# Eight transfers in place of sixteen for the turned shift, issued one key block sooner

## The chip, the cores and the metric

The program runs on one core of one Trainium2 chip. Its time is the device time of that core in microseconds (us). The core has a matrix engine (TensorE, PE in the profile), a vector engine (VectorE, DVE), a scalar engine (ScalarE, ACT), GpSimd (POOL) and a queue that does nothing but issue transfers (SyncE, SP). SBUF is the core's on-chip memory with 128 partitions, PSUM its accumulator memory with eight banks.

## The reference, cut to what matters

```
x = x + attention(layernorm(x))      # 2 sequences x 2048 tokens x 256, 16 heads of 16
x = x + experts(layernorm(x))        # router, 2 of 4 experts per token

scores = Q @ K^T / 4
A = softmax(scores)
out = (0.6 * A + 0.4 * L) @ V        # L: a fixed band of 7 neighbours
out = out @ Wo^T + bo
```

The change touches the attention alone, of which there are 2 x 16 = 32 heads with 2048 x 2048 scores each. The softmax needs the largest score of every query, so that the exponential is taken of score minus maximum.

## The kernel before, in words

The 32 heads are worked one after the other, each as 16 key blocks of 128 keys (`kb` in the code). For one head and one key block TensorE computes four chunks of scores, each 128 keys x 512 queries (L748), ScalarE takes their exponential into `probs` (L696), and TensorE multiplies with the values (L760). Scores lie with keys on the partitions, and so the maximum of a query cannot be subtracted there by a per-partition operand. It goes into the matmul: the stack `score_q` has three times 16 rows of query pieces and two more rows (rows 48 and 49) with minus the maximum of each query, in a high and a low piece; `score_k` holds ones in those rows. Two copies of the stack lie in the partitions from 0 and from 64 (`ROW_TILES = 2`, `ROW_TILE = 64`): queries 0 to 1023 in the first, 1024 to 2047 in the second.

The maxima are found one head ahead, from a second set of scores with queries on the partitions: TensorE fills two banks (L738), VectorE reduces them (L638), two reductions a key block. Maxima run `LOOK - ST` = 5 blocks ahead of the scores, so that the 16 blocks of head n+1 are done in the key block `kb == 10` of head n. There VectorE writes `neg_max` (L646), GpSimd splits it into `shift` (L604, L606), and at `kb == SHIFT_AT` VectorE turns it with 32 x 32 transposes into `shift_tok` (L654). SyncE then moves pieces of `shift_tok` into the two extra rows of `score_q` (L493); it is 128 bytes from each of some partitions of `shift_tok` to one row. TensorE waits for all of it before the first scores of the next head, which it computes in `kb == 15` (the wait on `shift_in`, L814).

SyncE's queue is in order. For head n it goes: loads of the maximum stacks for head n+2 (L528), the gather of head n's softmax sums (L530, 4 transfers by L147), a pad, a weight chunk's store and load, the inverse of the sums out and back (L536 to L538), the head's result (L540), the shift of head n+1 (L543), and, after the last scores of head n (`s_ready`, L545), the loads of the score stacks for head n+2 (L546), 12 transfers like the maximum stacks' 12. VectorE inverts the gathered sums in `kb == INVERT_AT` = 3 of the next head (L658), in the midst of its reductions. The queues of all engines are written out by hand in this order; a loop body holds six heads.

Of the kernel before, what the change touches and what calls it, by code (L numbers as in the profile page):

```python
# [7 lines left out]
F32 = mybir.dt.float32  # L8
# [8 lines left out]
P = 128  # L17
# [9 lines left out]
ST = SEQ // P  # L27
# [7 lines left out]
PIECES = 2  # L35
# [3 lines left out]
STACK = HD * len(Q_ROWS)  # L39
SROWS = STACK + PIECES  # L40
ROW_TILES = 2
ROW_TILE = P // ROW_TILES
# [3 lines left out]
WIN = P + 2 * WINDOW  # L46
BAND = BT * WIN + 2 * WINDOW
LOOK = 21
SHIFT_AT = 12
INVERT_AT = 3  # L50
PROBS = 4
SIX = 6
QUAD = 32
# [29 lines left out]
def ds(start, size):  # L83
    return bass.ds(start, size)


def by_head(engine, body):

    rounds = (NHEADS - 1) // SIX
    with engine.Fori(0, rounds) as i:  # L90
        for k in range(SIX):
            body(SIX * i + k, SIX // 2 * i + k // 2, k, False)
    for n in range(rounds * SIX, NHEADS):
        body(n, n // 2, n - rounds * SIX, n == NHEADS - 1)
# [24 lines left out]
def load_max(sp, dram, q_stack, k_stack, n, signal):  # L119
    load_stack(sp, dram, 0, Q_ROWS, q_stack, n, False, signal)  # L120
    load_stack(sp, dram, 1, K_ROWS, k_stack, n, True, signal)


def load_score(sp, dram, q_stack, k_stack, n, signal):
    load_stack(sp, dram, 0, Q_ROWS, q_stack, n, True, signal)
    load_stack(sp, dram, 1, K_ROWS, k_stack, n, False, signal)
# [17 lines left out]
def gather_sums(sp, keep, signal):  # L144

    for c in range(BPS):
        sp.dma_start(keep["sum_tok"][QUAD * c:QUAD * (c + 1), :],  # L147
                     keep["heads_sb"][QUAD * c + HD:QUAD * c + HD + 1, :].rearrange("o (t q) -> o t q", q=ST)
                     ).then_inc(signal, 16)


def store_inverse(sp, dram, keep, signal):

    sp.dma_start(dram["inv"].rearrange("(p t) -> p t", t=ST), keep["inv_tok"][:]).then_inc(signal, 16)


def spread_inverse(sp, dram, keep, signal):

    for c in range(BPS):
        row = dram["inv"][c * BLOCK:(c + 1) * BLOCK].rearrange("(o f) -> o f", o=1)  # L160
        sp.dma_start(keep["inv_rows"][QUAD * c:QUAD * c + HD, :], row.partition_broadcast(HD)).then_inc(signal, 16)


def store_head(sp, dram, keep, place, signal):

    for c in range(BPS):
        sp.dma_start(dram["o"][ds(place, 1), :, c * BLOCK:(c + 1) * BLOCK].squeeze(0),
                     keep["heads_sb"][QUAD * c:QUAD * c + HD, :]).then_inc(signal, 16)


def load_heads(sp, dram, keep, i, signal):

    b, q0 = i // BPS, (i % BPS) * BLOCK
    for m in range(KD):
        head = 1 + b * HEADS + m * (HEADS // KD)
        sp.dma_start(keep["o_block"][i % 2][:, m, :],
                     dram["o"][head:head + HEADS // KD, :, q0:q0 + BLOCK].rearrange("h d t -> (h d) t")
                     ).then_inc(signal, 16)
# [215 lines left out]
def attend(nc, ctx, dram, keep, block):  # L394
# [8 lines left out]
    def sb(name, shape, dt=F32):  # L403
        return ctx.enter_context(nc.sbuf_tensor(name, shape, dt))

    def sem(name):
        return ctx.enter_context(nc.semaphore(name))
# [4 lines left out]
    score_q = [sb(f"score_q{u}", [STACK_ROWS, SPLIT], F32R) for u in range(2)]  # L412
# [8 lines left out]
    part_max, neg_max, shift, shift_tok = (keep[n] for n in ("part_max", "neg_max", "shift", "shift_tok"))  # L421
# [11 lines left out]
    def count_of(n, kb, c):  # L433
        return n * UNITS + CH * kb + c + 1

    def bank_of(k, kb, c):

        return ps_s[(k * UNITS + CH * kb + c) % RING]
    SHIFT_DMAS = PIECES * ROW_TILES * P // QUAD
    PARTS = 2  # L440

    ones_set = sem("ones_set")
# [10 lines left out]
    shift_in = [sem(f"shift_in{u}") for u in range(2)]  # L453
# [30 lines left out]
    @block.sync  # L484
    def _(sp):
        def load_shift(u):

            for q in range(P // QUAD):
                for c in range(PIECES):
                    for h in range(ROW_TILES):  # L490
                        row, first = h * ROW_TILE + STACK + c, QUAD * q + c * ST + h * ST // ROW_TILES
                        to = score_q[u][row:row + 1, :].bitcast(F32).rearrange("o (t q i) -> o t q i", q=P // QUAD, i=QUAD)
                        sp.dma_start(to[:, :, q, :], shift_tok[first:first + ST // ROW_TILES, :]  # L493
                                     ).then_inc(shift_in[u], 16)

        load_max(sp, dram, max_q[1], max_k[1], 1, max_in[1])
        sp.wait_ge(ones_set, SCORE_ONES)
        load_score(sp, dram, score_q[0], score_k[0], 0, score_in[0])
        load_score(sp, dram, score_q[1], score_k[1], 1, score_in[1])
        for dst, src in ((w_o[:], dram["woT"].rearrange("(k p) n -> p k n", p=P)),  # L500
                         (w_r1[:], dram["rW1"].rearrange("(k p) n -> p k n", p=P)),
                         (w_r2[:], dram["rW2"].rearrange("(k p) n -> p k n", p=P)),
                         (b_r1[:], dram["rb1"]),
                         (bias_o[:], dram["bo"].rearrange("(o f) -> o f", o=1).partition_broadcast(P))):
            sp.dma_start(dst, src).then_inc(route_in, 16)
        sp.wait_ge(shift_tr, 1)
        load_shift(0)
        sp.dma_start(keep["band"][:], dram["band"][0]).then_inc(keep["band_in"], 16)

        def load_chunk(n):  # L510
            sp.dma_start(w_raw[:], dram["we"][ds(n, 1)].squeeze(0)).then_inc(w_in, 16)

        def store_chunk(n):
            sp.wait_ge(w_lo, n + 1)
            sp.dma_start(dram["w_split"][ds(n, 1)].squeeze(0), w_pair[:].bitcast(F32)).then_inc(w_stored, 16)

        def pad_slots(n):
            sp.dma_start(dram["xs"][ds(n * SLOTS, SLOTS), :], dram["pads"]).then_inc(pads_in, 16)

        pad_slots(NHEADS)  # L520
        sp.dma_start(dram["out"][TOKENS:, :], dram["pads"][:, 0:DIM]).then_inc(pads_in, 16)
        load_chunk(0)

        def body(n, h, k, last):
            u, more = k % 2, not isinstance(n, int) or n + 2 < NHEADS
            if more:
                sp.wait_ge(m_ready, 2 * ST * (n + 1))
                load_max(sp, dram, max_q[u], max_k[u], n + 2, max_in[u])  # L528
            sp.wait_ge(o_copied, n + 1)
            gather_sums(sp, keep, sums_in)  # L530
            pad_slots(n)
            store_chunk(n)
            if not last:
                load_chunk(n + 1)
            sp.wait_ge(inv_ready, n + 1)
            store_inverse(sp, dram, keep, inv_out)  # L536
            sp.wait_ge(inv_out, 16 * (n + 1))
            spread_inverse(sp, dram, keep, inv_in)  # L538
            sp.wait_ge(scaled, n + 1)
            store_head(sp, dram, keep, n, o_out)  # L540
            if not last:
                sp.wait_ge(shift_tr, n + 2)
                load_shift(1 - u)  # L543
            if more:
                sp.wait_ge(s_ready, count_of(n, ST - 1, CH - 1))  # L545
                load_score(sp, dram, score_q[u], score_k[u], n + 2, score_in[u])  # L546

        by_head(sp, body)
        sp.wait_ge(o_out, 16 * BPS * NHEADS)
        for i in range(2):  # L550
            load_heads(sp, dram, keep, i, keep["heads_in"][i])
# [81 lines left out]
    def _(dve):  # L633
# [7 lines left out]
        def split_shift(m, u):  # L641

            dve.wait_ge(m_read, 2 * ST * (m + 1))
            if not isinstance(m, int) or m > 0:
                dve.wait_ge(shift_ready, m)
            nc.vector.tensor_reduce(neg_max[:], part_max[:, u], axis=AXIS.X, op=ALU.max, negate=True  # L646
                                    ).then_inc(shift_step, 1)

        def transpose_shift(m, loaded, loads):

            dve.wait_ge(shift_ready, m + 1)
            if loaded is not None:
                dve.wait_ge(loaded, 16 * SHIFT_DMAS * loads)
            nc.vector.transpose(shift_tok[:], shift[:].rearrange("p c t -> p (c t)").bitcast(F32)).then_inc(shift_tr, 1)  # L654
# [17 lines left out]
        def body(n, h, k, last):  # L672
            u = k % 2
            for kb in range(ST):
# [5 lines left out]
                if ahead == ST - 1 and not last:  # L680
                    split_shift(n + 1, 1 - u)
                if kb == SHIFT_AT and not last:
                    transpose_shift(n + 1, shift_in[u], h + 1)
# [47 lines left out]
    def _(pe):  # L731
# [52 lines left out]
        for t in range(LOOK):  # L784
# [3 lines left out]
            for p in range(2):  # L788
                half = 2 * t + p
                maxima(t, t % ST, t // ST, p)  # L790
                if half == FIRST_SCORES:
                    pe.wait_ge(v_copied, BANKS - 1)
                    pe.wait_ge(score_in[0], 16 * STACK_DMAS)
                    pe.wait_ge(shift_in[0], 16 * SHIFT_DMAS)
                if half >= FIRST_SCORES:
# [5 lines left out]
        def body(n, h, k, last):  # L801
            u = k % 2
            pe.wait_ge(v_in, n + 1)
            for kb in range(ST):
# [7 lines left out]
                if kb == ST - 1 and more_scores:  # L812
                    pe.wait_ge(score_in[1 - u], 16 * STACK_DMAS * (h + 1 + u))
                    pe.wait_ge(shift_in[1 - u], 16 * SHIFT_DMAS * (h + 1 + u))  # L814
                if more_scores:
# [929 lines left out]
```

## Time and profile before

| | |
|---|---|
| time, median of 3 runs | 2596.38 us (2569.75 to 2608.95) |
| profiled execution | 2588.01 us, span 2586.2 us |
| TensorE busy | 2261.4 us (87%) |
| VectorE busy | 1641.1 us (63%) |
| ScalarE busy | 1351.8 us (52%) |
| mean granted TensorE clock | 0.806 of full |

The span is the time from the first to the last instruction of the profiled execution. Busy time counts an engine's own instructions; what it waits for stands in the view of waits, and the granted clock of a stretch in the view by windows (1.00 is 2.4 GHz, 0.50 is 1.2 GHz). The heads take up most of the span: the shift is turned for the first at 118.4 us and for the last at 1941.8 us. What follows them is the output projection, the router and the experts.

### The profile page before, as it was taken

How to read it: one execution, taken by the hardware profiler on the slowest of the kernel's cores; microseconds unless marked ns; L12 is line 12 of the kernel's file. 1: busy time of each engine (PE TensorE's matmuls, PEld its weight loads, DVE VectorE, ACT ScalarE, POOL GpSimd, SP SyncE). 2: the span in 40 equal slices, each digit the busy share in tenths (PEclk: the TensorE clock that was granted, in tenths of full speed). 3: DMA queues.
4: the chain of work that ended last, by engine and by line, in shares of the span. 5: the costliest groups of instructions: out<-in, count | busy, mean ns of one | idle time of the engine just before them, and what ended most of it. 6: DMA issues, size and time to landing. Idle time of an engine off the chain costs nothing. (4 is left out here: it accounts for less than half of the span.)

```text
span 2586.2 us, 48018 instructions
## 1 busy us (share of the span) xinstructions
PE 2261.4 (87%) x16092; PEld 1100.5 (43%) x16092; DVE 1641.1 (63%) x2123; ACT 1351.8 (52%) x2390; POOL 367.9 (14%) x380
## 2 busy tenths in 40 slices
PE   8988888888887888888887888888889699999998
PEld 4532333232232233322332332322332577999997
DVE  6766667566577676766776666676770377655554
ACT  3255666456566565665665555565666144222322
POOL 1440000000000000000000000000000046222222
PEclk9977778667688777887877677786876799999999
DMA  7723443233333354333333333443311237778885
GB/s 250 179 72 74 75 91 70 62 65 63 63 63 63 74 86 82 71 65 64 63 63 64 62 68 74 75 92 64 66 45 38 70 126 282 230 236 272 283 275 147
DMA packets 133884, 279.86 MB, mean 108 GB/s; under 512 B 43616, under 2 KB 74336, under 8 KB 126944
## 3 DMA queue, kind: packets, MB, share of 16 engines
q1 hardware_dynamic: 120464, 258.65, 40.0%
q0 software_dynamic: 13152, 17.83, 3.5%
q8 instruction: 144, 2.36, 0.4%
q14 instruction: 124, 1.02, 0.2%
HBM read 215.40 MB, written 78.54 MB: 114 GB/s over the span
## 5 line engine op out<-in xcount | busy, mean ns | idle before, releaser
L638 DVE TENSOR_REDUCE part_max<-psum 128x1 f32<-128x1024 f32 x1024 | 1242.2, 1221 | 584.1 <-PE psum L738 579.0
L696 ACT ACTIVATE probs<-psum 128x512 f32<-128x512 f32 x2048 | 1114.1, 595 | 739.0 <-PE psum L748 690.7
L748 PE MATMUL psum<-score_q,score_k 50*128 50x512 f32 x2048 | 923.2, 543 | 256.7 <-DMA score_q<-shift_tok 245.6
L738 PE MATMUL psum<-max_k,max_q 48*128 48x512 f32 x2048 | 895.3, 536 | 16.1 <-DVE part_max L638 16.0
L760 PE MATMUL psum<-probs,v_ones 128*32 128x256 f32 x8192 | 819.8, 480 | 0.5 <-ACT probs L696 0.2
L748 PEld LDWEIGHTS psum<-score_q,score_k 50*128 50x128 f32 x2048 | 379.1, 229 | 828.2 <-ACT probs L696 545.9
L760 PEld LDWEIGHTS psum<-probs,v_ones 128*32 128x32 f32 x8192 | 177.3, 119 | 474.6 <-issue 366.0
L738 PEld LDWEIGHTS psum<-max_k,max_q 48*128 48x128 f32 x2048 | 358.6, 226 | 32.8 <-DVE part_max L638 24.1
L1154 ACT ACTIVATE x_sb<-psum,x_sb 128x512 f32<-128x512 f32 (+1 forms) x160 | 101.5, 635 | 253.9 <-PE psum L1550 253.8
L1569 PE MATMUL psum<-w,h_hi 128*128 128x256 f32 x1120 | 203.0, 280 | 0.0
L1569 PEld LDWEIGHTS psum<-w,h_hi 128*128 128x128 f32 x1120 | 179.4, 189 | 10.3 <-DVE h_lo L1365 0.2
L1569 PE MATMUL psum<-w,h_lo 128*128 128x256 f32 x560 | 156.4, 279 | 0.0
L1363 DVE CAST h_hi<-x_sb 128x512 fp32r<-128x512 f32 (+1 forms) x160 | 66.6, 416 | 129.1 <-ACT x_sb L1154 128.8
L611 POOL TENSOR_TENSOR heads_sb<-heads_sb,inv_rows 128x512 f32<-128x512 f32 x32 | 40.9, 1278 | 640.0 <-DMA inv_rows<-inv 640.0
L1569 PEld LDWEIGHTS psum<-w,h_lo 128*128 128x128 f32 x560 | 105.6, 189 | 0.0
L1365 DVE TENSOR_TENSOR h_lo<-x_sb,h_hi 128x512 fp32r<-128x512 f32 (+1 forms) x160 | 100.3, 627 | 5.5
L572 POOL COPY v_ones<-v_sb 128x256 f32<-128x256 f32 x32 | 12.7, 396 | 629.6 <-PE psum L760 629.5
L1550 PE MATMUL psum<-xT_hi,w 128*128 128x512 f32 (+1 forms) x320 | 93.9, 375 | 2.2 <-ACT x_sb L1154 2.2
L1550 PE MATMUL psum<-route_xT_hi,w 128*128 128x512 f32 (+1 forms) x320 | 90.3, 364 | 0.0
L1102 POOL DMA_INDIRECT out<-x_sb,token x36 | 56.8, 1578 | 136.5 <-DVE x_sb L1383 82.0
L1102 POOL DMA_INDIRECT out<-attnT,token x34 | 53.4, 1570 | 140.2 <-DVE attnT L1383 92.7
L1074 POOL DMA_INDIRECT xs<-xrow,slot_at x64 | 63.3, 990 | 22.6 <-issue 18.4
(177 smaller groups left out, 1250.8 us busy)
## 6 DMA issues: line engine op xcount, KB each, us to landing
w<-w_split SPq DMA_DIRECT2D x40, 2048.0 KB, 8.5
max_q<-qk_pieces SPq DMA_DIRECT2D x192, 128.0 KB, 6.9
score_k<-qk_pieces SPq DMA_DIRECT2D x192, 128.0 KB, 4.6
xs<-in_pads SPq DMA_DIRECT2D x33, 528.0 KB, 5.6
qk_pieces<-pieces SPq DMA_DIRECT2D x32, 512.0 KB, 4.8
w_split<-w_pair SPq DMA_DIRECT2D x32, 512.0 KB, 6.1
max_k<-qk_pieces SPq DMA_DIRECT2D x192, 64.0 KB, 7.9
score_q<-qk_pieces SPq DMA_DIRECT2D x192, 64.0 KB, 2.2
```

What stands on the lines that cost most here:

```text
L638: nc.vector.tensor_reduce(part_max[:, u, t, p:p + 1], ps_m[p].rearrange("q b f -> q (b f)"), axis=AXIS.X, op=ALU.max).then_inc(m_read, 1)
L696: nc.scalar.activation(probs[:, kb % PROBS, chunk * BLOCK:(chunk + 1) * BLOCK], bank_of(k, kb, c), ACT.Exp, scale=float(HD) ** -0.5).then_ ...
L738: last = nc.tensor.matmul(ps_m[p][:, h, :], max_q[u][rows, t * P:(t + 1) * P], max_k[u][rows, p * BLOCK:(p + 1) * BLOCK], start=True, stop ...
L748: nc.tensor.matmul(bank_of(k, kb, c), score_k[u][rows, kb * P:(kb + 1) * P], score_q[u][rows, part * BLOCK:(part + 1) * BLOCK], start=True ...
L760: last = nc.tensor.matmul(ps_o[QUAD * j:QUAD * (j + 1), at:at + BLOCK // PARTS], v_ones[u][:, kb, :], probs[:, kb % PROBS, j * BLOCK + at: ...
L1074: nc.gpsimd.indirect_dma_start(dram["xs"], bass.IndirectOffsetOnAxis(ap=at, axis=0), xrow[i % XROWS][:, t, :], None).then_inc(scattered[i ...
L1102: nc.gpsimd.indirect_dma_start(dram["out"], bass.IndirectOffsetOnAxis(ap=token[i % TOKEN_SETS][:, t:t + 1], axis=0), y[u][:, t, :], None, ...
L1154: nc.scalar.activation(h[m % H][:, 0:n], ps_h[m % PS_H][:, 0:n], ACT.Gelu, bias=biases[i % 2][:, m:m + 1]).then_inc(gelu_done, 1)
L1363: nc.vector.tensor_copy(h_hi[m % HALVES][:, 0:n], h[m % H][:, 0:n]).then_inc(h_hi_ready, 1)
L1365: nc.vector.tensor_tensor(h_lo[m % HALVES][:, 0:n], h[m % H][:, 0:n], h_hi[m % HALVES][:, 0:n].bitcast(F32), ALU.subtract).then_inc(h_lo_r ...
L1550: last = nc.tensor.matmul(ps_h[m % PS_H][:, 0:n], w[u][:, 2 * k + m // 4, c, at:at + P], xx[:, k, 0:n], start=j == 0, stop=j == len(terms) ...
L1569: last = nc.tensor.matmul(ps_y[u][:, t // 2, (t % 2) * DIM:(t % 2 + 1) * DIM], hs[m % HALVES][:, toks], w[u][:, chunk, c, at:at + DIM], st ...
```

## The change

`load_shift` issues one transfer for each of four quarters `q` and two pieces `c`, in place of one for each of `q`, `c` and half `h`. A transfer now reads 16 partitions of `shift_tok` and writes 8 pieces of 32 numbers into each of two rows, which lie 64 partitions apart. `SHIFT_DMAS`, the count that is waited for, follows. `SHIFT_AT` goes from 12 to 11.

```diff
-SHIFT_AT = 12
+SHIFT_AT = 11
...
-    SHIFT_DMAS = PIECES * ROW_TILES * P // QUAD
+    SHIFT_DMAS = PIECES * P // QUAD
...
             for q in range(P // QUAD):
                 for c in range(PIECES):
-                    for h in range(ROW_TILES):
-                        row, first = h * ROW_TILE + STACK + c, QUAD * q + c * ST + h * ST // ROW_TILES
-                        to = score_q[u][row:row + 1, :].bitcast(F32).rearrange("o (t q i) -> o t q i", q=P // QUAD, i=QUAD)
-                        sp.dma_start(to[:, :, q, :], shift_tok[first:first + ST // ROW_TILES, :]
-                                     ).then_inc(shift_in[u], 16)
+                    first = QUAD * q + c * ST
+                    to = score_q[u][STACK + c:STACK + c + ROW_TILE + 1:ROW_TILE, :].bitcast(F32).rearrange(
+                        "h (t q i) -> h t q i", q=P // QUAD, i=QUAD)
+                    sp.dma_start(to[:, :, q, :], shift_tok[first:first + ST, :]).then_inc(shift_in[u], 16)
```

On VectorE, in the body of a head from the last maximum of the next head on, it stood before:

```order
193 L646 TENSOR_REDUCE neg_max<-part_max 128x16
194 L637 ISA
195 L638 TENSOR_REDUCE part_max<-psum 128x1
196 L637 REGISTER_ALU
197 L638 TENSOR_REDUCE part_max<-psum 128x1
198 L637 ISA
199 L638 TENSOR_REDUCE part_max<-psum 128x1
200 L637 REGISTER_ALU
201 L638 TENSOR_REDUCE part_max<-psum 128x1
202 L654 STREAM_TRANSPOSE shift_tok<-shift 128x32
```

and at the same place now (all line numbers after the loop are one less):

```order
193 L645 TENSOR_REDUCE neg_max<-part_max 128x16
194 L636 ISA
195 L637 TENSOR_REDUCE part_max<-psum 128x1
196 L636 REGISTER_ALU
197 L637 TENSOR_REDUCE part_max<-psum 128x1
198 L653 STREAM_TRANSPOSE shift_tok<-shift 128x32
199 L636 ISA
200 L637 TENSOR_REDUCE part_max<-psum 128x1
201 L636 REGISTER_ALU
202 L637 TENSOR_REDUCE part_max<-psum 128x1
```

Two reductions of maxima stand between `neg_max` and the turn in place of four.

On SyncE, from the end of one head's result to the next loads, before:

```order
129 L167 DMA o<-heads_sb 16x512
130 L493 DMA score_q<-shift_tok 1x8x32 [waits shift_tr]
131 L493 DMA score_q<-shift_tok 1x8x32 x15
132 L545 ISA
133 L115 DMA score_q<-qk_pieces 16x1024 [waits s_ready]
```

and now:

```order
129 L167 DMA o<-heads_sb 16x512
130 L493 DMA score_q<-shift_tok 2x8x32 [waits shift_tr]
131 L493 DMA score_q<-shift_tok 2x8x32 x7
132 L544 ISA
133 L115 DMA score_q<-qk_pieces 16x1024 [waits s_ready]
```

Nothing else in the queue changes its place; the loads behind the shift keep their wait for the head's last scores.

## Rows read from the trace of the kernel before

**Rows 1.** The page's first line.

```profile
span 2586.2 us, 48018 instructions
```

**Rows 2.** Windows: stretch, length, busy (count) by engine, PEclk, DMA share, GB/s.

```profile
179.96:1941.85 1761.89, 1500.06 (x11482) 523.53 (x11480) 1171.31 (x1048) 1059.26 (x1945) 117.57 (x181) 0.75 0.36 69
2186.30:2586.00 399.70, 388.56 (x2678) 359.12 (x2676) 231.34 (x463) 113.82 (x173) 115.35 (x76) 0.99 0.77 241
1018.92:1034.40 15.48, 15.48 (x90) 5.00 (x92) 8.57 (x7) 7.96 (x15) 1.50 (x2) 0.50 1.01 167
1049.00:1062.00 13.00, 13.00 (x128) 4.90 (x132) 12.94 (x14) 11.42 (x22) 0.42 (x2) 1.00 0.01 2
```

**Rows 3.** Waits of the whole run: us in total, times, longest.

```profile
PE psum L748 <- DMA score_q<-shift_tok: 245.6, 31, 8.4
...
DVE inv_tok L658 <- DMA sum_tok<-heads_sb: 44.9, 13, 19.9
```

**Rows 4.** Line L654: durations ns min/median/max, first and last start.

```profile
L654 DVE STREAM_TRANSPOSE shift_tok<-shift x32: 200/201/211, 118.4 to 1941.8; 128x32 f32<-128x32 f32 x32
```

**Rows 5.** Timeline of TensorE: start, length, engine, line, tiles, count.

```profile
1004.63 0.39 PE L748 MATMUL psum<-score_q,score_k 50*128 50x512 f32 x1
...
1013.60 0.78 PE L748 MATMUL psum<-score_q,score_k 50*128 50x512 f32 x1 [8.00 <-DMA score_q<-shift_tok]
...
1018.03 0.79 PE L748 MATMUL psum<-score_q,score_k 50*128 50x512 f32 x1
...
1020.19 0.79 PE L748 MATMUL psum<-score_q,score_k 50*128 50x512 f32 x1
```

**Rows 6.** Timeline of VectorE, the same head.

```profile
1001.27 0.20 DVE L654 STREAM_TRANSPOSE shift_tok<-shift 128x32 f32<-128x32 f32 x1
...
1036.08 17.27 DVE L638 TENSOR_REDUCE part_max<-psum 128x1 f32<-128x1024 f32 x14 [0.29 <-PE psum L738]
1053.38 0.19 DVE L646 TENSOR_REDUCE neg_max<-part_max 128x16 f32<-128x32 f32 x1
...
1058.16 0.20 DVE L654 STREAM_TRANSPOSE shift_tok<-shift 128x32 f32<-128x32 f32 x1
```

**Rows 7.** Timeline of GpSimd, the second piece of the split.

```profile
1053.90 0.22 POOL L606 TENSOR_TENSOR shift<-neg_max,shift 128x16 fp32r<-128x16 f32 x1
```

**Rows 8.** Timeline of SyncE's issues, the same head.

```profile
1001.50 10.82 SPq L493 DMA_DIRECT2D score_q<-shift_tok  x16
1012.52 3.06 SPq L115 DMA_DIRECT2D score_q<-qk_pieces  x6
```

**Rows 9.** Windows, columns as above: while the shift's transfers are issued.

```profile
1002.00:1012.30 10.30, 3.59 (x36) 1.19 (x36) 4.26 (x4) 3.46 (x7) 0.00 (x0) 0.79 0.01 1
```

**Rows 10.** Timelines of SyncE and VectorE, two later heads.

```profile
1125.42 2.73 SPq L115 DMA_DIRECT2D score_q<-qk_pieces  x6
...
1145.75 0.25 DVE L658 RECIPROCAL inv_tok<-sum_tok 128x16 f32<-128x16 f32 x1 [3.96 <-DMA sum_tok<-heads_sb]
...
1184.73 3.79 SPq L115 DMA_DIRECT2D score_q<-qk_pieces  x6
...
1209.63 0.25 DVE L658 RECIPROCAL inv_tok<-sum_tok 128x16 f32<-128x16 f32 x1 [2.45 <-DMA sum_tok<-heads_sb]
```

**Rows 11.** A short wait of VectorE, and windows after it and after 1145.75.

```profile
920.74 0.25 DVE L658 RECIPROCAL inv_tok<-sum_tok 128x16 f32<-128x16 f32 x1 [1.27 <-DMA sum_tok<-heads_sb]
...
923.40:942.00 18.60, 18.60 (x186) 6.96 (x184) 18.49 (x17) 16.15 (x31) 1.70 (x3) 1.00 0.07 17
...
1149.00:1158.80 9.80, 9.80 (x56) 3.20 (x58) 5.45 (x6) 4.97 (x10) 1.26 (x1) 0.50 0.12 28
```

**Rows 12.** Lines L493, L147 and L702: durations ns min/median/max.

```profile
L493 SPq DMA_DIRECT2D score_q<-shift_tok x512: 620/626/1159, 118.6 to 1952.2; - x171
...
L147 SPq DMA_DIRECT2D sum_tok<-heads_sb x132: 507/590/1949, 138.5 to 2019.0; - x132
...
L702 ACT ACTIVATE heads_sb<-psum x32: 597/597/598, 197.2 to 2011.9; 128x512 f32<-128x512 f32 x32
```

## The prediction, made before the changed kernel ran

> **What bounds the kernel now.** I read the page first, then the waits, then one head in the timelines, then windows for the clock. The span is 2586.2 us [rows 1] and the profiled execution took 2588.0, 1.8 more; it lies 0.3% under the median of the runs, 2596.4. The shift is turned 32 times, first at 118.4 and last at 1941.8 us [rows 4]: 31 heads of 58.8 us each, 1823 us in all. The change touches nothing else, so I take one head apart.
>
> The floor of a head is VectorE. With the clock high it runs 14 reductions of maxima in 17.27 us without a gap [rows 6], 1.234 each; 32 of them make 39.5 us a head. In such a stretch VectorE is busy 12.94 of 13.00 us [rows 2].
>
> What a head takes beyond 39.5 are waits and what follows them. TensorE waits 245.6 us in 31 times for the transfers of the shift [rows 3], 7.9 a head. VectorE waits 44.9 us in 13 times for the gathered sums; the longest of these, 19.9, is in the last head, which has no maxima left and loses nothing by it, so 25.0 remain, 0.8 a head. That leaves 58.8 - 39.5 - 7.9 - 0.8 = 10.6 us a head.
>
> These 10.6 are the clock. Over the heads it is 0.75 on average, while the experts at the end run at 0.99 with TensorE busy 389 of 400 us [rows 2]: the clock is not lost to hard work. After the wait of 8.00 us, TensorE is busy all the time from 1018.92 to 1034.40, and at 0.50 [rows 2, 5]. A half key block then takes 1020.19 - 1018.03 = 2.16 us [rows 5] in place of 1.234: low-clock time loses 43% of itself. As a check: 0.75 means half of 58.8 us at the low level, 29; some 5 of them lie in the wait itself, and 24 x 0.43 = 10.3.
>
> Waits for the sums let the clock fall too, if they are long. After 1.27 us it stays at 1.00, after 3.96 it is 0.50 [rows 11]. Of the 13 waits seven in the heads are of 2.2 us or more (one stands there), and each of those was followed by a fall. So 31 + 7 falls share 31 x 10.6 = 329 us: **8.65 us a fall**.
>
> **The change, part by part.** I count from T, the start of the turn.
>
> *Fewer transfers.* 16 take 10.82 us to issue [rows 8], 0.676 apart. What one costs with twice the pieces no row shows. Bounds: from below the quickest issue of the other transfer from SBUF to SBUF, 0.51; from above twice the present one, 1.35. The gather of the sums has 32 pieces in place of 8 and takes 0.59 in the median against 0.63 [rows 12], so the count of pieces doesn't set the price, and I take 0.676 as now: 8 x 0.676 = 5.4 us. The transfers load nothing: the DMA share is 0.01 while they are issued [rows 9].
>
> A rule stands against this edit. The Trainium skill, DMA: Bandwidth & Descriptors, Rules for kernel authors, says that a DMA whose outermost dimension is small is confined to that many engines; the new destination starts with a 2, the old with an 8. By it each transfer would run on two engines and land later; with a share of 0.01 it changes my sum by nothing, and what it could do at worst is the slower rival below.
>
> *Turned sooner.* Two reductions fewer stand between, 2 x 1.234 = 2.5 us. It is not held up by GpSimd: the split ends at 1054.12, 0.74 after `neg_max` began [rows 6, 7], and the turn will come 4.78 - 2.5 = 2.3 after it.
>
> *TensorE's wait for the shift.* Now TensorE wants the shift at 1013.60 - 8.00 = 1005.60, T + 4.3 [rows 5, 6]; the last issue ends at T + 11.05 and TensorE goes on 1.3 later. With T 2.5 earlier it wants it at T + 6.8. The transfers are issued from T + 0.23 to T + 5.6 and there at T + 6.9. A wait of 0.1 us is left of 7.9.
>
> *What is late next: the sums.* Behind the shift SyncE issues 24 loads, then the gather. The DMA engines are the limit there (share 1.01 [rows 2]), so the sums land a fixed time after the first load: 1145.75 - 1125.42 = 20.3 us where VectorE was waiting for them. The heads that begin a turn of SyncE's loop take longer, 1209.63 - 1184.73 = 24.9 [rows 10]. The first load waits for the head's last scores, which end at 1005.02 [rows 5], T + 3.75 now and T + 6.2 then; so loads start at T + 6.3 and the sums are there at T + 26.6. VectorE has 16 reductions and the turn between T and its inverse, 16 x 1.234 + 0.1 = 19.9 us. It now waits 6.7 us in a head. Today it has the 8 us wait and the low clock to hide behind. Five heads of 31 wait 4.6 more, 0.7 on average: 7.5. I take 7.6 for the spread of landings.
>
> *The clock.* A wait of 6.7 us is above those that let it fall [rows 11]. TensorE fills two banks and then stands as well. One fall a head, 8.65 us, at another place; the second falls are gone.
>
> *ScalarE's copy of the result,* 0.60 us [rows 12], now comes in the low-clock stretch after the shift wait and costs nothing. With the cover gone it lies in a stretch where ScalarE is 11.42 of 13.00 busy [rows 2]: between 0 and 0.6, I take 0.3.
>
> The sum for a head: 39.5 + 0.1 + 7.6 + 8.65 + 0.3 = 56.15, 2.65 less than now. Over 31 heads 82 us, and about 5 from the last head, whose shift has 5.4 us less of issue ahead of it and no maxima to be late for. 2588 - 87 = **2501 us**; I say 2500. Against the median it is 3.7% less.
>
> **The rivals.**
>
> *The fall does not come.* If TensorE, which has scores and values to work on beside the maxima, keeps its clock through the wait at the sums, 31 x 8.65 = 268 us more are won: 2233. Against it stands the fall after a wait of 3.96 at this very place [rows 11]. Chance 0.05.
>
> *The price is by the piece.* With 1.35 us a transfer the issue takes 10.8 us as before, and only the earlier turn is left: TensorE waits 12.3 - 6.8 = 5.5, the clock falls there, and at the low clock VectorE comes to its inverse after the sums, as today. 31 x 2.45 = 76 less: 2512. Hardly another time, but another picture. Chance 0.10.
>
> *No change that can be measured.* The waits exchange places, 7.9 + 0.8 against 7.7, and the whole gain is the seven second falls and a little more. If a fall at the sums costs the whole 10.6, because the clock comes back later there, a head takes 58.1: 31 x 0.7 + 5 = 27 less, 2561. For it speaks that single falls differ widely: one at the shift lasted until 1034 [rows 2]. Chance 0.20.
>
> *Slower.* The price of a transfer to two rows far apart, on fewer engines, is higher than any here. From 8 x 1.66 = 13.3 us of issue on, the earlier turn is eaten up (10.8 + 2.5). At 1.95, the slowest issue of the gather [rows 12], it is 15.6: the shift is there at T + 17.1, TensorE waits 10.3 in place of 7.9, and the sums stay hidden. 31 x 2.4 = 74 more: 2662. The place is SyncE's queue at the shift. Against it: 132 issues of the gather at 0.59 in the median, with four times the pieces [rows 12]. Chance 0.05.
>
> **How the numbers follow.** The forecast holds 0.60. About 2% is what a measurement of this kernel can tell from no change, 52 us: below 2544 is faster. Of my own case nearly all lies there (0.55), of the price by the piece 0.09, the fall that does not come 0.05, and a quarter of the no-change case 0.05: faster 0.74. Slower is its rival and a little of the no-change case, where the clock stays low longer still: 0.06. The rest, 0.20, is the same. For the range: fixed landing times 2 us shorter give 2440; the no-change rival is at 2561. 2440 to 2560 leaves out the two far rivals and the edge of the third.
>
> **What would show it.** In the waits, TensorE behind the transfers of the shift falls from 245.6 to under 40 us, with 0.1 to 1 each; VectorE behind the sums rises from 44.9 to some 230 to 260, 6 to 8 each. SyncE issues eight transfers in 5.0 to 5.8 us. The first load comes 6.3 us after the turn, and the sums 20 to 21 us after that. The granted clock over the heads goes from 0.75 to about 0.77 to 0.80, and it falls in the key blocks 3 and 4 of a head, not at 15. TensorE still waiting 5 us or more for the shift would be the price by the piece; a wait at the sums with the clock at 1.00 after it would be the big gain. The forecast is wrong if the sums land much sooner or later than 20 us after the first load, or if a fall costs another amount than 8.65 us.

## The result, and the profile after

| | before | changed |
|---|---|---|
| median of 4 runs | 2594.20 us | 2404.57 us |
| lowest to highest | 2569.75 to 2608.95 | 2363.93 to 2412.85 |
| profiled execution | 2588.01 us | 2412.85 us |
| mean granted TensorE clock, profiled | 0.806 | 0.847 |

The ratio is 0.920, with a 95% interval from 0.901 to 0.940; a kernel's executions scatter by some 2% here, and the ratio is formed from the fast ones of each alone, so it lies a little under the ratio of the two medians, 0.927. The changed kernel is 8% faster, where 3.7% was forecast, and lies below the range of 2440 to 2560 us. The profiled execution of the changed kernel is the longest of its four, 8 us over their median; the accounts below are of that one against the profiled one of before, 2411.1 us of span against 2586.2 [rows 1], 175 us less.

The waits of the changed kernel (us in total, times, longest). All line numbers are one less than before. The last line is TensorE at the four jumps back of the loop; "issue" means that the profile shows nothing that ended the wait.

```profile
DVE inv_tok L657 <- DMA sum_tok<-heads_sb: 177.1, 30, 14.0
...
PE psum L737 <- DVE part_max L637: 139.0, 30, 7.4
...
PE psum L747 <- issue: 12.7, 4, 3.3
```

The wait of TensorE for the shift, 245.6 us in [rows 3], is gone from the list. In its place VectorE waits for the sums, 177.1 against 44.9, and TensorE behind VectorE. The turn and the transfers by their lines (durations ns min/median/max):

```profile
L653 DVE STREAM_TRANSPOSE shift_tok<-shift x32: 199/201/213, 117.5 to 1787.6; 128x32 f32<-128x32 f32 x32
...
L493 SPq DMA_DIRECT2D score_q<-shift_tok x256: 495/495/717, 117.8 to 1791.8; - x128
```

The 31 stretches from turn to turn, called heads from here on (what follows the last turn is the last head), now take 1670.1 us, 53.9 each, against 58.8 by [rows 4]: 153 of the 175 us. A transfer with twice the pieces takes 0.495 us to issue against 0.626 [rows 12].

One head, VectorE first, then SyncE, then TensorE, from its turn on (start, length, engine, line, tiles, count, idle time before and what ended it):

```profile
1031.14 0.20 DVE L653 STREAM_TRANSPOSE shift_tok<-shift 128x32 f32<-128x32 f32 x1
1031.27 11.02 DVE L637 TENSOR_REDUCE part_max<-psum 128x1 f32<-128x1024 f32 x9
1042.64 8.62 DVE L637 TENSOR_REDUCE part_max<-psum 128x1 f32<-128x1024 f32 x7 [0.35 <-PE psum L737]
1057.68 0.25 DVE L657 RECIPROCAL inv_tok<-sum_tok 128x16 f32<-128x16 f32 x1 [6.42 <-DMA sum_tok<-heads_sb]
```

```profile
1031.37 4.44 SPq L493 DMA_DIRECT2D score_q<-shift_tok  x8
1037.39 2.73 SPq L115 DMA_DIRECT2D score_q<-qk_pieces  x6
...
1050.20 2.47 SPq L147 DMA_DIRECT2D sum_tok<-heads_sb  x4
```

```profile
1059.08 0.80 PE L737 MATMUL psum<-max_k,max_q 48*128 48x512 f32 x2 [5.62 <-DVE part_max L637]
```

Read it against the prediction's T: transfers issued in 4.44 us, first load at T + 6.25 (forecast 6.3), sums there at T + 26.5 (26.6), a wait of 6.4 us (6.7). Windows of the same kernel (columns as in [rows 2]): all heads, this head after the wait, and head 30.

```profile
117.55:1787.62 1670.07, 1511.27 (x11840) 531.92 (x11839) 1213.99 (x1085) 1086.66 (x2004) 147.89 (x193) 0.79 0.38 75
...
1062.00:1080.00 18.00, 18.00 (x104) 5.79 (x104) 10.03 (x9) 9.34 (x18) 1.27 (x1) 0.50 0.06 12
...
1749.19:1787.62 38.43, 38.16 (x370) 14.10 (x368) 37.03 (x34) 33.81 (x64) 3.98 (x7) 1.00 0.35 75
```

The clock over the heads rises from 0.75 [rows 2] to 0.79. In the head shown the fall now comes with the wait at the sums; in this execution each head from the second to the thirtieth has one fall.

### The profile page after: what moved, and what is told of

Read it like the earlier page. It is cut to its first block and busy times, and to the rows that moved or that the text cites. A ratio compares the mean times of both kernels' runs of the same rounds, so it can differ in the third digit from the quotient of the medians.

```text
span 2411.1 us, 47762 instructions
## 1 busy us (share of the span) xinstructions
PE 2199.5 (91%) x16092; PEld 1086.9 (45%) x16092; DVE 1640.5 (68%) x2123; ACT 1346.0 (56%) x2390; POOL 369.2 (15%) x380
## 5 line engine op out<-in xcount | busy, mean ns | idle before, releaser
L737 PE MATMUL psum<-max_k,max_q 48*128 48x512 f32 x2048 | 866.2, 525 | 139.0 <-DVE part_max L637 139.0
L747 PE MATMUL psum<-score_q,score_k 50*128 50x512 f32 x2048 | 886.0, 518 | 12.7 <-issue 12.7
L759 PE MATMUL psum<-probs,v_ones 128*32 128x256 f32 x8192 | 782.4, 460 | 8.0 <-ACT heads_sb L701 7.6
L747 PEld LDWEIGHTS psum<-score_q,score_k 50*128 50x128 f32 x2048 | 364.3, 218 | 550.3 <-ACT probs L695 523.5
L737 PEld LDWEIGHTS psum<-max_k,max_q 48*128 48x128 f32 x2048 | 347.9, 219 | 160.2 <-DVE part_max L637 152.7
L657 DVE RECIPROCAL inv_tok<-sum_tok 128x16 f32<-128x16 f32 x32 | 8.1, 252 | 177.1 <-DMA sum_tok<-heads_sb 177.1
L603 POOL CAST shift<-neg_max 128x16 fp32r<-128x16 f32 x31 | 6.1, 198 | 490.3 <-DVE neg_max L645 490.3
```

The lines of the kernel that those rows point to most:

```text
L737: last = nc.tensor.matmul(ps_m[p][:, h, :], max_q[u][rows, t * P:(t + 1) * P], max_k[u][rows, p * BLOCK:(p + 1) * BLOCK], start=True, stop ...
L747: nc.tensor.matmul(bank_of(k, kb, c), score_k[u][rows, kb * P:(kb + 1) * P], score_q[u][rows, part * BLOCK:(part + 1) * BLOCK], start=True ...
L759: last = nc.tensor.matmul(ps_o[QUAD * j:QUAD * (j + 1), at:at + BLOCK // PARTS], v_ones[u][:, kb, :], probs[:, kb % PROBS, j * BLOCK + at: ...
```

## The experiments

Each kernel below was executed four times, and the profile is of one execution. The first four were measured beside executions of the kernel before with a median of 2582.67 us, the last four beside others with 2575.59 us; at the result above it was 2594.20. So some 10 to 20 us of a difference between two sets may belong to the sets.

**The two edits apart.** First the merged transfers with the turn where it was:

```diff
-SHIFT_AT = 11
+SHIFT_AT = 12
```

> Eight transfers, but the shift is still turned in key block 12. Theory (TensorE's wait at the shift gives way to VectorE's wait at the sums): the last issue ends 4.7 us after the turn as in the changed kernel, so TensorE waits about 1.7 us a head for the shift; the first load starts 4.9 us after the turn, the sums are there 20 us later, and VectorE waits about 6 us for them with a fall of the clock. A head takes 1 to 2 us more than with both edits: 2430 to 2460 us. Rival (the clock falls after the 1.7 us already, so that the low clock hides the wait at the sums): waits at the sums under 2 us a head and a head of 52 to 54 us, 2340 to 2390.

Measured: 2373.59 us (2357.07 to 2400.93), ratio to before 0.920 (0.909 to 0.930). This is the rival's time, and the same ratio as with both edits. The waits, and for one head TensorE's wait for the shift and the window after it:

```profile
DVE inv_tok L657 <- DMA sum_tok<-heads_sb: 88.1, 22, 14.0
...
PE psum L747 <- DMA score_q<-shift_tok: 47.3, 29, 3.7
```

```profile
270.42 0.56 PE L747 MATMUL psum<-score_q,score_k 50*128 50x512 f32 x1 [1.62 <-DMA score_q<-shift_tok]
```

```profile
272.50:290.00 17.50, 17.50 (x102) 5.72 (x98) 9.78 (x9) 9.28 (x17) 2.22 (x3) 0.50 0.97 158
```

A wait of 1.6 us for the shift is left, and after it the clock stands at 0.50. In 20 of the 30 heads it fell there, 6 to 8 us after the turn; in 15 of the 20 there was no other fall in the head, and VectorE, held back by the low clock, then waited at most 1.2 us for the sums; in five there were two falls. In the other ten it fell later, at the sums or at the loop's turn. The theory had a wait of 6 us at the sums in every head; in all heads but the last it is 74 us together, 2.4 a head, where the rival said under 2. So the theory fails here, and the rival holds in half of the heads: a short wait at the shift brings the fall early, and the low clock then hides the late sums, so that a head costs no more than one with the wait at the sums.

Then the earlier turn with the 16 transfers of before:

```diff
-SHIFT_AT = 12
+SHIFT_AT = 11
```

> The 16 transfers of before, turned in key block 11. Theory: TensorE still waits 5.5 us a head for the shift (7.9 less 2.45), the clock falls there and hides the sums as before; a head takes 2.4 us less than before, 2594 - 76 = 2518 us. Rival (the earlier turn does all of the gain): 2410.

Measured: 2477.31 us (2464.63 to 2497.34), ratio 0.963 (0.953 to 0.973). Its waits:

```profile
PE psum L748 <- DMA score_q<-shift_tok: 168.6, 31, 6.1
...
DVE inv_tok L658 <- DMA sum_tok<-heads_sb: 41.8, 12, 19.9
```

168.6 / 31 = 5.4 us for the shift, as forecast. The time is 41 us below the expectation, 2518 (12 of them lie between the two sets of the kernel before), and far from the rival's. So the merge alone gives 8%, the earlier turn alone 4%, and both together no more than the merge.

**Is the wait at the sums all that is left?** The changed kernel with the inverse three key blocks later:

```diff
-INVERT_AT = 3
+INVERT_AT = 6
```

> The changed kernel with VectorE's inverse of the sums in key block 6 in place of 3 (INVERT_AT). Theory (the wait at the sums and the fall after it are all that is left above 39.5 us a head): VectorE comes to the inverse 27.3 us after the turn, later than the sums at 26.5, so wait and fall are gone; 25 heads take about 40 us in place of 55.3, the four at a turn of the loop about 50; 2405 - 385 = 2020 us, TensorE's clock near 0.95. Rival (the clock is low for the load of the work or for the loop's turns, not for this wait): the waits go and the clock stays near 0.8; 2405 less 29 times 6 = 2230 us or more.

Measured: 2033.95 us (2027.81 to 2037.59), ratio 0.789 (0.783 to 0.796), 14 us from the theory. All heads and one head in its windows, and that head on VectorE:

```profile
117.79:1413.45 1295.66, 1273.30 (x11840) 466.91 (x11839) 1215.01 (x1086) 1084.07 (x2004) 147.87 (x193) 0.96 0.49 97
455.54:495.54 40.00, 39.73 (x390) 14.64 (x392) 39.21 (x37) 35.14 (x66) 3.94 (x6) 1.00 0.52 101
```

```profile
455.54 0.20 DVE L653 STREAM_TRANSPOSE shift_tok<-shift 128x32 f32<-128x32 f32 x1
455.67 11.08 DVE L637 TENSOR_REDUCE part_max<-psum 128x1 f32<-128x1024 f32 x9
467.09 16.10 DVE L637 TENSOR_REDUCE part_max<-psum 128x1 f32<-128x1024 f32 x13 [0.35 <-PE psum L737]
483.11 0.24 DVE L657 RECIPROCAL inv_tok<-sum_tok 128x16 f32<-128x16 f32 x1
...
495.54 0.20 DVE L653 STREAM_TRANSPOSE shift_tok<-shift 128x32 f32<-128x32 f32 x1
```

40.0 us from turn to turn, VectorE busy 39.2 of them, TensorE's clock full. Only VectorE's waits at the sums (one of 14.0, behind the last turn, is left) and the falls after them stood between 55 and 40. Of the 25 heads from the second to the thirtieth that lie at no turn of the loop, 24 took 39.8 to 40.0 us without a fall, so it is not the load of the work that takes the clock there. The exception is the second, 47.4 us: at its start VectorE waits 3.4 us for GpSimd's split of the shift, TensorE stops for 2.7, and the clock falls. In the changed kernel it is the same (3.5 and 2.7), so in this one place the earlier turn is held up by GpSimd after all.

The same edit on the kernel before:

> The kernel before with the inverse in key block 6. Theory: its wait for the shift (8 us) and the fall there stay; 25 us of waits at the sums and seven second falls of 8.65 us go: 2594 - 85 = 2509 us. Rival (second falls cost little, since the clock would be low for other reasons): 2594 - 25 = 2569.

Measured: 2505.89 us (2472.87 to 2538.96), ratio 0.967 (0.954 to 0.980): 77 us less than before had beside it (2582.67), where the theory said 85. Its waits:

```profile
PE psum L748 <- DMA score_q<-shift_tok: 244.7, 31, 8.5
...
DVE inv_tok L658 <- DMA sum_tok<-heads_sb: 19.9, 1, 19.9
```

The interval means 51 to 118 us less. It leaves out the rival's 25, and fits a second fall at the prediction's price without measuring that price closely. The later inverse alone is worth 77 us where TensorE still waits for the shift, and some 360 where it does not (371 between the two medians, 12 of which lie between the two sets of the kernel before).

**Or is it the order on SyncE?** The changed kernel with the gather ahead of the loads:

```diff
@@ body(n), SyncE
-            sp.wait_ge(o_copied, n + 1)
-            gather_sums(sp, keep, sums_in)
             pad_slots(n)
...
                 load_shift(1 - u)
+                sp.wait_ge(o_copied, n + 2)
+                gather_sums(sp, keep, sums_in)
             if more:
```

and one gather ahead of the first body. (What the body of head n gathers and VectorE inverts in it are the sums of head n-1, whose result ScalarE has copied by then; the account of SyncE's queue ahead of the prediction calls them head n's.)

> The changed kernel with the gather of the sums issued ahead of the 24 loads in place of behind them (inverse in key block 3 as before). Theory (the sums are late because the loads stand ahead of them): they are there some 14 us after the turn, VectorE, which comes at 19.9, waits for nothing, and the heads take 40 us as with the later inverse: about 2035 us. Rival (the inverse's way back and the head's result now queue behind the loads, and the next shift is late for it): waits for the shift come back, 2150 us or more.

Measured: 2126.73 us (2098.34 to 2153.98), between the theory and the rival. No wait for the sums is left but the last head's, as the theory says; the rival holds in part, for the result's way back stands behind the loads now. In the head that is turned at 571.0 us SyncE sends the inverse at 598.13, straight behind the last load, and can read it back only at 606.24; in the changed kernel with the later inverse that way took 2.2 us in the head shown (483.38 to 485.59). So GpSimd scales the head late and splits the shift late, and the turn waits:

```profile
DVE inv_tok L659 <- DMA sum_tok<-heads_sb: 14.0, 1, 14.0
```

```profile
598.13 0.49 SPq L154 DMA_DIRECT2D inv<-inv_tok  x1
606.24 1.73 SPq L161 DMA_DIRECT2D inv_rows<-inv  x4
```

```profile
609.52 1.28 POOL L612 TENSOR_TENSOR heads_sb<-heads_sb,inv_rows 128x512 f32<-128x512 f32 x1 [26.96 <-DMA inv_rows<-inv]
```

```profile
611.38 0.21 DVE L655 STREAM_TRANSPOSE shift_tok<-shift 128x32 f32<-128x32 f32 x1 [0.40 <-POOL shift L607]
```

```profile
DVE shift_tok L655 <- POOL shift L607: 38.8, 20, 4.4
...
PE psum L749 <- DMA score_q<-shift_tok: 8.2, 10, 1.9
```

In ten heads TensorE stopped for 0.9 to 3.7 us at such a late turn, and in each of the ten the clock fell.

**What is the earlier turn worth once the sums are out of the way?** Merged transfers, turn in block 12, inverse in block 6:

```diff
-SHIFT_AT = 11
-INVERT_AT = 3
+SHIFT_AT = 12
+INVERT_AT = 6
```

> Eight transfers, turned in key block 12, with the inverse in key block 6: what the sooner turn is worth once the sums are out of the way. Theory (a wait of 1.5 us for the shift is left in every head, and two in three of such waits were followed by a fall of the clock where only the transfers were merged): 40 + 1.5 + 0.65 x 8.65 = 47 us a head, 2034 + 25 x 7 = 2210 us. Rival (such a wait costs itself alone): 2034 + 40 = 2075.

Measured: 2209.82 us (2177.38 to 2227.55), on the theory's number.

```profile
PE psum L747 <- DMA score_q<-shift_tok: 48.4, 30, 3.2
```

With these 48.4 us of waits for the shift the time is 176 us over the run with the turn in block 11. From the second head to the thirtieth, those without a fall took 41.4 to 41.7 us and the 15 with one 45.7 to 63.8. That the time meets the theory is luck in part: it took two falls in three heads at 8.65 us each, and away from the loop's turns there were 10 in the 24 heads from the third on, at 9.3, but one at each of the four turns as well.

**The loop's turns.**

```diff
-SIX = 6
+SIX = 12
```

on the kernel with the later inverse.

> The changed kernel with the inverse in key block 6 and twelve heads in a loop body in place of six. Theory (each turn of the loop stops TensorE for 3 us, and the clock falls there; the four turns cost 5, 14, 11 and 16 us above 40 in the run with the later inverse): two turns fewer, 20 to 25 us less than 2034, 2010. Rival (twice the code costs as much in fetches elsewhere): 2034 or more.

Measured: 2001.87 us (1994.45 to 2015.33), ratio 0.778 (0.771 to 0.784): the fastest of all, and 8 us under the theory. TensorE has one stop of this kind left, 3.4 us. Three turns of the loop are gone, not two as I had counted, for there is one jump back left of four. The head at that jump takes 49.5 us, all others but the first two 38.3 to 40.1.

**How short a wait is harmless?**

```diff
-INVERT_AT = 3
+INVERT_AT = 5
```

> The changed kernel with the inverse in key block 5. Theory (the sums are there 26.5 us after the turn whatever VectorE does, which comes at 24.9): a wait of about 1.6 us a head, followed by a fall in some two heads of three, 2034 + 25 x (1.6 + 5.6) = 2215 us. Rival (a wait so short at this place is no reason for a fall, since TensorE still has scores to work on): 2034 + 40 = 2075.

Measured: 2109.68 us (2098.47 to 2121.53), ratio 0.818 (0.810 to 0.826), nearer the rival. VectorE waited 34.5 us in 22 heads. Of the waits of up to 1.9 us one, of 1.72, was followed by a fall; of the six from 2.04 to 3.18, five were. A harmless one and a long one, and the windows after them:

```profile
1034.98 0.25 DVE L657 RECIPROCAL inv_tok<-sum_tok 128x16 f32<-128x16 f32 x1 [1.89 <-DMA sum_tok<-heads_sb]
...
1077.71 0.26 DVE L657 RECIPROCAL inv_tok<-sum_tok 128x16 f32<-128x16 f32 x1 [3.18 <-DMA sum_tok<-heads_sb]
```

```profile
1036.00:1047.00 11.00, 10.62 (x103) 3.98 (x106) 10.93 (x10) 8.37 (x16) 1.28 (x1) 1.00 0.14 38
1081.00:1094.00 13.00, 13.00 (x76) 4.19 (x72) 7.67 (x7) 6.51 (x12) 1.27 (x1) 0.50 0.08 21
```

## Why the prediction was wrong

The mechanism was right for a typical head: the wait at the shift goes, the wait at the sums takes its place, one fall stays. The size was wrong, 87 us forecast against 175 in the profiled executions. Step by step:

- **Issue of the transfers.** Forecast 5.4 us, measured 4.44 to 4.45. The price was taken as unchanged and fell by a fifth. It moved nothing: the loads behind wait for the head's last scores.
- **TensorE's wait for the shift.** Forecast 0.1 us, none measured.
- **Few engines per transfer,** the rule of the Trainium skill, DMA: Bandwidth & Descriptors, Rules for kernel authors, stood against the edit. Where TensorE was waiting, in the run with the merge alone, it went on 1.3 us after the last issue ended, as before, so nothing landed later; whether two engines carried the transfers no row shows.
- **The typical head.** Forecast 39.5 + 0.1 + 6.7 + 8.65 + 0.3, 55.3 without the extras. The 25 heads from the second to the thirtieth that lie at no turn of the loop took 55.26 on average. That the two agree so closely is partly luck: with the inverse later such a head takes 39.9 (39.5 + 0.1 + 0.3 here), so 15.3 are wait and fall, of which the wait is 6.2 for 6.7 forecast and the fall 9.1 for 8.65.
- **The step that failed is the last line of the sum, "Over 31 heads 82 us, and about 5 from the last head".** The step gives every head the typical head's cost, and a fall to all of them; and it gives the last head a gain from the shorter issue alone, with nothing for the fall there. Three kinds are not like the typical head:
  - *The first and the 31st head.* Behind the shift only 12 loads stand ahead of the gather, not 24: the score stacks' are missing in the first, the maximum stacks' in the 31st. There is no wait for the sums and no fall. They took 45.6 and 38.4 us, not 56.15: with the extra counted for the first, 31 us of the miss. SyncE in the 31st, turned at 1749.19:

```profile
1755.51 3.81 SPq L115 DMA_DIRECT2D score_q<-qk_pieces  x6
1759.42 2.68 SPq L115 DMA_DIRECT2D score_k<-qk_pieces  x6
1762.32 2.47 SPq L147 DMA_DIRECT2D sum_tok<-heads_sb  x4
```

  - *The four heads at a turn of the loop.* I counted 4.6 us of wait more for each. The sums did come later, some 31.6 us after the turn, but the heads took 51.1 us on average, less than the others; 36 us of the miss. TensorE stops there too:

```profile
449.94 0.65 PE L747 MATMUL psum<-score_q,score_k 50*128 50x512 f32 x1 [3.26 <-issue]
```

```profile
452.00:466.00 14.00, 14.00 (x80) 4.71 (x76) 7.63 (x7) 6.51 (x12) 0.00 (x0) 0.50 0.72 117
```

The clock falls at this stop, 13 to 14 us after the turn, and the low clock covers most of the lateness of the sums; VectorE waits 1.5 to 2.5 us. The Trainium skill, Runtime: NRT & Kernel Launch, Instruction fetch mechanics, says that a taken branch whose target lies outside the current window of code has to fetch it before execution goes on. The traces agree as far as they go: TensorE stops once at each of the four jumps back, for 3.0 to 3.3 us, and with twelve heads in a body once, at the one jump left; that it waits for code there no row shows. The kernel before had the stop as well, 1.3 to 1.8 us long and inside the low clock.

  - *The last head.* 21 us were gained behind the last turn, not 5. Before, TensorE stopped for 4.7 us there, up to 1.1 us after the last of the shift's transfers was issued, the clock fell, and it was low for 58 us, to the end of the head's work, which came 70.0 us after the turn. Now there is no such stop and no fall in the head, and it ends 45.5 us after the turn. (That is 24.5 us; what follows took 3.5 longer.) Of before and of the changed kernel, 40 us of this head each:

```profile
1960.00:2000.00 40.00, 40.00 (x232) 11.17 (x230) 0.25 (x1) 24.96 (x46) 1.27 (x1) 0.50 0.21 60
```

```profile
1800.00:1840.00 40.00, 35.52 (x320) 15.39 (x320) 0.25 (x1) 30.89 (x59) 1.56 (x6) 0.99 0.23 65
```

16 us of the miss. The 31 + 36 + 16, with 4 of the typical heads and 1 of the start and of rounding, make 88, from 2501 to 2413.

- **That short waits are harmless** was read out of one wait of 1.27 us [rows 11]. The trace has four more of up to 1.16 us, none followed by a fall, one of them in a clock that was low already. At the sums it nearly holds, up to 1.9 us. At the shift 1.5 us brought the fall in half of the heads and more, and at a late turn a stop of TensorE of 0.9 us did once. It did not move this forecast, but it is why the merge alone is as good as both edits.
- **The rivals.** "The fall does not come" did not happen. Its price for a fall, 8.65 us, is near the 9.1 above; but the fall goes not because TensorE keeps its clock through the wait, but only when the wait goes too, and then the head is at 40 us. The other three rivals were not met either: the transfers got cheaper, and the time is below all of theirs.

What stays open: why a low clock lasts 7 us in one head and 48 in another with TensorE busy nearly all the while. The spread of the runs goes with the clock (the shortest of the changed kernel, 2363.93 us, had 0.865 on average, the longest 0.847), but that it comes from this alone is not shown. That the earlier turn adds nothing to the merge rests on two ratios with intervals of 2 to 4%; a gain or loss of under 2% is not excluded.

## What to carry to other kernels

Work out the sum by kinds of head, not by one head times their number: the first, the last and those at a loop's jump have other queues before them. When one of two late arrivals is taken away, look at once at the second, for here it cost the clock as much as the first did. One constant, the key block of the inverse, was worth nearly twice the edit itself, and only after it.

## What the runs showed of the hardware

A transfer from SBUF to two rows with 16 pieces of 128 bytes is issued in 0.495 us, one to a single row with eight in 0.626. In the run with eight transfers, the turn in block 12 and the later inverse, TensorE stopped for 1.5 to 1.65 us at the shift in 29 heads, and in 15 of them its clock went from full to half; in the changed kernel a fall lasted 7 to 48 us. In the changed kernel with the later inverse a jump back in the loop stopped TensorE for about 3 us, and its head took 5 to 16 us more than the others, with the fall that follows.
